# Raw rows scattered straight from X, slots normalised where they are read, six shared groups ahead of the routed part

## The chip, the cores and the metric

One Trainium2 chip, one core of it. The metric is the device time of one execution in microseconds; the kernel before has a median of 673.12 us over 3 runs (672.82 to 673.82).

## The reference, cut to what matters

Two layers over x of shape (2, 2048, 256), float32. First an attention whose scores are distances of 3-component positions (16 heads share one score matrix), then a mixture-of-experts block, which is where the change lies:

```python
x = x + attention(layernorm(x))
xt = layernorm(x)                                   # 4096 rows of 256
scores = softmax(xt @ gate_w.T)                     # 8 experts
_, idx = top_k(scores + gate_bias, 2)
weights = take_along_axis(scores, idx)
for e in range(8):
    gate_e = sum(where(idx == e, weights, 0))
    h = silu(xt @ w1[e].T) * (xt @ w3[e].T)
    y = y + gate_e * (h @ w2[e].T)                  # the routed part
z = silu(xt @ sw1.T) * (xt @ sw3.T) @ sw2.T         # the shared part, inner width 512
x = x + y + z
```

## The kernel before, in words

The 4096 rows are 32 tiles of 128 rows. X, with one tile per index, stays in SBUF through both layers. Every product is made of three matmuls (high by high, high by low, low by high part), so every operand is split: ScalarE copies the rounded high part, VectorE subtracts it for the low part. Each engine has its own hand-written program; semaphores tie them, and within an engine the written order is the order of the work. The second layer has these stages, each named by what the engines' functions are called.

**Logits.** GpSimd makes constants; VectorE folds the statistics of 32 tiles (`mv`), ScalarE takes the square root (`std`), VectorE normalises four tiles at a time into XN (`logits_xn`, line 974 in the helper `normalised`). TensorE transposes XN (L1217), ScalarE and VectorE split the transposed tiles (L858, L985), TensorE multiplies by the gate and turns the result (L1234).

**Router.** VectorE runs a chain of small operations over [128, 32, 8] (from L1047): softmax, two picks, a count per expert, and the slot of every row. Each operation waits for the one before (`done`). Then `choice_weights` gathers the two weights of a row into `meta`.

**Shared part ahead.** A group is four tiles (512 rows) and has four steps n, one per 128 of the inner width. In step n TensorE does `products(n)` (12 matmuls of 512 columns), then `outputs(n - 1)` (12 of 256 columns), and once per group the transposes of the next group (L1258, 8 matmuls). ScalarE does silu (`sg`), the high part of h (L891), and for n < 16 the high part of one of the 16 pieces of the experts' weights (W_hi, L911). VectorE does h (`hf`, L1138), its low part (`h_lo`, L1149), the low part of W (`W_lo`, L1153), and once per group four normalisations (XN), two low parts (XT_lo, L1019) and two additions of the shared output to X (`add_shared`, L1129). HALF = 5 groups run before the routed part. Between `hf` and `h_lo` VectorE also prepares one or two tiles for the scatter (`scatter_tile`): it normalises a tile into a buffer XR (L974) and copies two extra columns, home row and weight (L1108); ScalarE copies the row for the second choice (`second_row`, L898). GpSimd scatters each to DRAM by an indirect DMA (L827), 64 in all, into `slots_in`, where rows of one expert lie in tiles of 128 slots.

**Routed part.** 71 slot tiles. SP loads one into XS (four buffers, next load when TensorE has transposed it and GpSimd has copied its two columns, L833 and L834). TensorE transposes it (L1329), multiplies by the two gate matrices, transposes h (L1345), and multiplies by the third; ScalarE and VectorE split and combine (L933, L1183, L929, L1179, L924, L1174); ScalarE writes the weighted result (L941), GpSimd scatters it home (L843).

**Tail.** SP loads both routed results of every row into YG (L789, 16 DMAs); the remaining 3 groups of the shared part run (12 steps). In seven of their steps, between `hf` and `h_lo`, VectorE adds the two routed results of a group to each other (L1116, two operations) and to X (L1121, two operations): `add_routed`; the eighth group is added at the very end. SP writes tiles out (L794).

The lines that set the split of the work:

```python
HALF = 5
def tiles_to_scatter(n):
    return range(min(2 + 5 * n // 3, NT), min(2 + 5 * (n + 1) // 3, NT))
def group_to_add(n):
    return {2: [0], 3: [1], 4: [2], 5: [3], 6: [4], 7: [5], 9: [6]}.get(n - MC * HALF, [])
```

## Time and profile before

| | |
|---|---|
| median of 3 runs | 673.12 us |
| the profiled execution, its time | 675.16 us |
| its span, first to last instruction | 673.4 us |
| mean granted TensorE clock | 0.921 of full |
| TensorE matmul busy | 560.7 us, 83% |
| VectorE busy | 448.1 us, 67% |
| ScalarE busy | 338.5 us, 50% |
| GpSimd busy | 216.4 us, 32% |

The stages in the trace, in us from the start of the span: attention to 260, logits and router to 319, shared part ahead to 425, routed part to 608, tail to the end. "Idle before" in brackets is how long the engine had nothing to do ahead of a row, and the releaser is what ended that. A matmul's end is modelled, and neighbouring matmuls overlap, so the distance between two starts says what one costs.

### The profile page before, as it was taken

The numbers are of one execution on the slowest core, as the hardware profiler recorded it, in microseconds if no ns is written. First come the engines' busy times: TensorE is split into PE (matmuls) and PEld (weight loads), VectorE is DVE, ScalarE is ACT, GpSimd is POOL, SyncE is SP. The second block draws the span as 40 slices with busy tenths as digits, with TensorE's granted clock in tenths as the row PEclk, the third lists the DMA queues.
The fourth block names the chain that finished last, engine by engine and source line by source line (L and its number), as shares of the span: only waits on it lengthen the run. The fifth ranks groups of instructions, "written<-read, shape, count | busy, mean of one in ns | idle before, by whom it ended". The sixth has DMA issues, their size and how long they took to land.

```text
span 673.4 us, 11259 instructions
## 1 busy us (share of the span) xinstructions
PE 560.7 (83%) x3484; PEld 485.8 (72%) x3484; DVE 448.1 (67%) x1143; ACT 338.5 (50%) x710; POOL 216.4 (32%) x404
## 2 busy tenths in 40 slices
PE   3738899965698994952797989899999999998995
PEld 2727489964658994541676777688888888887884
DVE  4984997888399765967775775444444444444985
ACT  0416998333499851641444444355555555553331
POOL 3061300034132001001774776154545545452000
PEclk9778999968797997977797999899999999999998
DMA  8988000000000004700221222233333333325941
GB/s 280 318 249 3 1 1 1 2 1 0 1 0 1 2 1 149 320 1 8 87 96 55 83 92 87 72 103 103 104 111 103 103 104 104 110 80 174 385 162 62
DMA packets 57127, 62.59 MB, mean 93 GB/s; under 512 B 14736, under 2 KB 50448, under 8 KB 57072
## 3 DMA queue, kind: packets, MB, share of 16 engines
q1 hardware_dynamic: 49216, 43.46, 22.7%
q0 software_dynamic: 6480, 17.77, 7.4%
q10 hardware_dynamic: 1376, 0.66, 0.4%
q8 instruction: 31, 0.51, 0.3%
q14 instruction: 24, 0.20, 0.1%
HBM read 30.50 MB, written 31.37 MB: 92 GB/s over the span
## 4 chain that ended last, share of the span: by engine, by line
PE 40%; DVE 11%; issue 4%; ACT 4%; DVEq 1%; another core or an unknown queue 1%; POOL 0%; ACTq 0%; POOLq 0%
PE bank L1208 11%; PE bank L1210 11%; PE bank L1209 11%; PE bank L1329 2%; PE bank L1345 2%; DVE hf L1138 2%; PE bank L1217 1%; ACT h_hi L891 1%; DVE X L1129 1%; DVE XR L974 1%; DVE h_lo L1149 1%; ACT W_hi L911 1%; DVE XN L974 1%; DVE W_lo L1153 1%; DVE XT_lo L1019 1%
## 5 line engine op out<-in xcount | busy, mean ns | idle before, releaser
L843 POOL DMA_INDIRECT token_out<-YS,to_row x71 | 69.6, 980 | 96.6 <-ACT YS L941 93.0
L827 POOL DMA_INDIRECT slots_in<-XR,slot x64 | 69.4, 1085 | 88.1 <-DVE XR L1108 69.8
L575 PE MATMUL a_bank<-VO,E_hi 128*128 128x258 f32 x272 | 78.6, 289 | 6.6 <-DVE E_lo L482 6.6
L579 PE MATMUL a_bank<-VO,E_lo 128*128 128x258 f32 x272 | 78.2, 288 | 0.0
L577 PE MATMUL a_bank<-VO,E_hi 128*128 128x256 f32 x272 | 78.0, 287 | 0.0
L1179 DVE TENSOR_TENSOR hr<-bank,sr 128x256 f32<-128x256 f32 x71 | 30.1, 425 | 62.0 <-issue 48.9
L1208 PE MATMUL bank<-XT_hi,sw_hi 128*128 128x512 f32 x128 | 53.6, 419 | 13.2 <-DVE XT_lo L1019 11.6
L1208 PE MATMUL bank<-W_hi,XST_hi 128*128 x142 | 62.3, 438 | 0.5 <-DVE XST_lo L1183 0.5
L929 ACT ACTIVATE sr<-bank 128x256 f32<-128x256 f32 x71 | 27.2, 383 | 64.2 <-PE bank L1210 63.4
L575 PEld LDWEIGHTS a_bank<-VO,E_hi 128*128 128x128 f32 x272 | 52.9, 194 | 7.3 <-DVE E_lo L482 7.3
L1210 PE MATMUL bank<-W_hi,XST_lo 128*128 x142 | 56.9, 401 | 0.0
L1209 PE MATMUL bank<-W_lo,XST_hi 128*128 x142 | 56.7, 399 | 0.0
L1208 PE MATMUL bank<-sw_hi,h_hi 128*128 128x256 f32 x128 | 37.5, 293 | 22.7 <-DVE h_lo L1149 18.0
L1183 DVE TENSOR_TENSOR XST_lo<-bank,XST_hi 128x256 fp32r<-128x256 f32 x71 | 30.1, 424 | 38.0 <-ACT XST_hi L933 37.9
L453 DVE TENSOR_SCALAR E<-a_bank 128x512 f32<-128x512 f32 (+3 forms) x80 | 41.6, 598 | 20.5 <-PE a_bank L565 20.5
L579 PEld LDWEIGHTS a_bank<-VO,E_lo 128*128 128x128 f32 x272 | 52.9, 194 | 0.0
L577 PEld LDWEIGHTS a_bank<-VO,E_hi 128*128 128x128 f32 x272 | 52.8, 194 | 0.0
L1210 PE MATMUL bank<-XT_hi,sw_lo 128*128 128x512 f32 x128 | 52.5, 410 | 0.0
L1209 PE MATMUL bank<-XT_lo,sw_hi 128*128 128x512 f32 x128 | 52.4, 409 | 0.0
L482 DVE TENSOR_TENSOR E_lo<-E,E_hi 128x512 fp32r<-128x512 f32 (+1 forms) x80 | 46.0, 603 | 3.9 <-ACT E_hi L299 3.9
L1208 PE MATMUL bank<-W_hi,hT_hi 128*128 x142 | 45.8, 323 | 0.1
L1208 PEld LDWEIGHTS bank<-sw_hi,h_hi 128*128 128x128 f32 x128 | 24.7, 193 | 27.9 <-DVE h_lo L1149 22.2
(227 smaller groups left out, 1621.3 us busy)
## 6 DMA issues: line engine op xcount, KB each, us to landing
XS<-slots_in SPq DMA_DIRECT2D x71, 129.0 KB
YG<-token_out SPq DMA_DIRECT2D x16, 512.0 KB, 7.7
slots_in<-blank SPq DMA_DIRECT2D x7, 1161.0 KB, 14.6
W_raw<-in_wT_dram SPq DMA_DIRECT2D x8, 768.0 KB, 12.5
X<-in_x_dram SPq DMA_DIRECT2D x8, 512.0 KB, 7.7
out_dram<-X SPq DMA_DIRECT2D x32, 128.0 KB, 2.3
token_out<-YS,to_row POOLq DMA_INDIRECT x71, 2.4
slots_in<-blank SPq DMA_DIRECT2D x1, 1032.0 KB, 14.6
```

The costliest lines, as they stand in the source:

```text
L453: dve.tensor_scalar(blk, Q_ps[n % NQ][:, 0:w], 0.0, None, ALU.max).then_inc(s_e2, 1)
L482: dve.tensor_tensor(E_lo[:, n % NE, 0:w], blk, E_hi[:, n % NE, 0:w].bitcast(f32), ALU.subtract).then_inc(s_el, 1)
L575: pe.matmul(O_ps[Q % 2][j][:, 0:D + 2], E_hi[:, n % NE, cols], VO[:, kt, 0:D + 2], start=(kt == 0), stop=False)
L577: pe.matmul(O_ps[Q % 2][j][:, 0:D], E_hi[:, n % NE, cols], VO[:, kt, D + 2:VW], start=False, stop=False)
L579: mm = pe.matmul(O_ps[Q % 2][j][:, 0:D + 2], E_lo[:, n % NE, cols], VO[:, kt, 0:D + 2], start=False, stop=(kt == qt))
L827: pool.indirect_dma_start(out=xs, out_offset=bass.IndirectOffsetOnAxis(ap=slot[k][:, t:t + 1], axis=0), in_=XR[:, t % 4, k, :], in_offset= ...
L843: pool.indirect_dma_start(out=ys, out_offset=bass.IndirectOffsetOnAxis(ap=to_row[:, i:i + 1], axis=0), in_=YS[:, i % NYS, :], in_offset=No ...
L1179: dve.tensor_tensor(hr[:, v, :], S_ps[v][:, D:2 * D], sr[:, v, :], ALU.mult).then_inc(s_hr, 1)
L1183: dve.tensor_tensor(XST_lo[:, v, :, :], XT_ps[v][:, 0:D].rearrange("p (c n) -> p c n", c=KC), XST_hi[:, v, :, :].bitcast(f32), ALU.subtrac ...
L1208: pe.matmul(out, a_hi, b_hi, start=start, stop=False, **kw)
L1209: pe.matmul(out, a_hi, b_lo, start=False, stop=False, **kw)
L1210: return pe.matmul(out, a_lo, b_hi, start=False, stop=stop, **kw)
```

## The change

1. A row of X becomes 262 columns wide: 256 of data, then mean, reciprocal deviation, number of the first choice (FIRST), home row (HOME), second weight (W1), difference of the weights (DW). VectorE fills these in the router. GpSimd scatters rows of X itself, raw, twice; XR, `scatter_tile`, `second_row` and `meta` are gone.
2. The logits are made of raw X: TensorE transposes X, and the router corrects the logits by mean, the sum of the gate's columns (`gsum`, two small matmuls) and the reciprocal deviation. `logits_xn` is gone, the loops over the groups are written out on TensorE and VectorE, and the square root stands behind the first two groups on ScalarE. The choice weights are made before the slots are announced.
3. In the routed part VectorE normalises a slot tile into XSN and compares FIRST with the tile's expert (`slot_rows`: three operations, 71 times); GpSimd makes home row and weight of it by four small operations where there were two.
4. HALF = 6. Two groups are left for the tail. GpSimd adds the two routed results of a row (16 operations of 128x512), VectorE only adds that sum to X. Groups 5 and 6 are both added in the last step.

```diff
-RW = D + 2
+RW = D + 6
+MEAN, RSTD, FIRST, HOME, W1, DW = range(D, RW)
...
-        HALF = 5
+        HALF = 6
...
-            return {2: [0], 3: [1], 4: [2], 5: [3], 6: [4], 7: [5], 9: [6]}.get(n - MC * HALF, [])
+            return {2: [0], 3: [1], 4: [2], 5: [3], 6: [4], 7: [5, 6]}.get(n - MC * HALF, [])
...
 SyncE
             for i in range(4, NSLOT):
-                sp.wait_ge(s_xsT, i - 3)
+                sp.wait_ge(s_sn, i - 3)
                 sp.wait_ge(s_mt, 2 * (i - 3))
...
 GpSimd
             for t in range(NT):
                 for k in range(TOPK):
-                    if k == 0:
-                        pool.wait_ge(s_xr, 2 * t + 2)
-                    else:
-                        pool.wait_ge(s_xr1, t + 1)
                     pool.indirect_dma_start(out=xs,
                                             out_offset=bass.IndirectOffsetOnAxis(ap=slot[k][:, t:t + 1], axis=0),
-                                            in_=XR[:, t % 4, k, :], in_offset=None).then_inc(s_sc[t % 4], 16)
+                                            in_=X[:, t, :], in_offset=None).then_inc(s_sc[t // GT], 16)
 
             def meta_of(i):
+                row = XS[:, i % 4, :]
                 pool.wait_ge(s_xs[i % 4], 16 * (i // 4) + 16)
-                pool.tensor_copy(to_row[:, i:i + 1], XS[:, i % 4, D:D + 1]).then_inc(s_mt, 1)
-                pool.tensor_copy(by_weight[:, i:i + 1], XS[:, i % 4, D + 1:RW]).then_inc(s_mt, 1)
+                pool.wait_ge(s_sel, 2 * i + 2)
+                pool.tensor_tensor(home[:, i:i + 1], back[:, i:i + 1], row[:, HOME:HOME + 1], ALU.add).then_inc(s_meta, 1)
+                pool.tensor_tensor(by_weight[:, i:i + 1], is_first[:, i:i + 1], row[:, DW:DW + 1], ALU.mult)\
+                    .then_inc(s_meta, 1)
+                pool.wait_ge(s_meta, 2 * i + 2)
+                pool.tensor_copy(to_row[:, i:i + 1], home[:, i:i + 1]).then_inc(s_mt, 1)
+                pool.tensor_tensor(by_weight[:, i:i + 1], by_weight[:, i:i + 1], row[:, W1:W1 + 1], ALU.add)\
+                    .then_inc(s_mt, 1)
...
+            for g in range(NG):
+                pool.wait_ge(s_yg[g], 16 * TOPK)
+                for h in range(0, GT, 2):
+                    tiles = slice(g * GT + h, g * GT + h + 2)
+                    pool.tensor_tensor(YG[:, tiles, 0, :], YG[:, tiles, 0, :], YG[:, tiles, 1, :], ALU.add)\
+                        .then_inc(s_yy, 1)
...
 VectorE, router
             dve.wait_ge(s_lg, NG + 2)
+            done(dve.tensor_tensor(tmp[:, :, :], mv[:, :, 0:1].to_broadcast([P, NT, NX]), over_t(gsum), ALU.mult))
+            done(dve.tensor_tensor(logit[:, :, :], logit[:, :, :], tmp[:, :, :], ALU.subtract))
+            done(dve.tensor_tensor(logit[:, :, :], logit[:, :, :], over_e(rstd), ALU.mult))
...
+            for k, out in ((1, X[:, :, W1]), (0, X[:, :, DW])):
+                done(dve.tensor_tensor(tmp[:, :, :], pick[k][:, :, :], score[:, :, :], ALU.mult))
+                done(dve.tensor_reduce(out, tmp[:, :, :], AX.X, ALU.add))
+            done(dve.tensor_tensor(X[:, :, DW], X[:, :, DW], X[:, :, W1], ALU.subtract))
+            dve.wait_ge(s_cols, 3)
             dve.sem_inc(s_slot, 1)
...
 VectorE, add_routed and add_shared
-                dve.wait_ge(s_yg[g], 16 * TOPK)
                 dve.wait_ge(s_zf, 2 * g + 2)
                 for h in range(0, GT, 2):
                     tiles = slice(g * GT + h, g * GT + h + 2)
-                    dve.tensor_tensor(YG[:, tiles, 0, :], YG[:, tiles, 0, :], YG[:, tiles, 1, :], ALU.add)\
-                       .then_inc(s_yy, 1)
-                for h in range(0, GT, 2):
-                    tiles = slice(g * GT + h, g * GT + h + 2)
                     dve.wait_ge(s_yy, g * 2 + h // 2 + 1)
...
+                dve.wait_ge(s_sc[G], 16 * TOPK * GT)
...
 VectorE, routed part
+            def slot_rows(i):
+                dve.wait_ge(s_xs[i % 4], 16 * (i // 4) + 16)
+                if i >= 2:
+                    dve.wait_ge(s_xsT, i - 1)
+                row = XS[:, i % 4, :]
+                dve.tensor_scalar(XSN[:, i % 2, :], row[:, 0:D], row[:, MEAN:MEAN + 1], row[:, RSTD:RSTD + 1],
+                                  ALU.subtract, ALU.mult).then_inc(s_sn, 1)
+                dve.tensor_scalar(is_first[:, i:i + 1], row[:, FIRST:FIRST + 1], which[:, i:i + 1], None,
+                                  ALU.is_equal).then_inc(s_sel, 1)
+                dve.tensor_scalar(back[:, i:i + 1], row[:, FIRST:FIRST + 1], which[:, i:i + 1], -float(P * NT),
+                                  ALU.is_equal, ALU.mult).then_inc(s_sel, 1)
...
+            slot_rows(0)
             for i in range(-3, NSLOT):
+                if i + 4 < NSLOT:
+                    slot_rows(i + 4)
                 if i + 3 < NSLOT:
                     tokens_lo(i + 3, (i + 3) % 2)
```

How the rows move, at three places. First VectorE in a step of the shared part ahead that also normalises the next group (XR is the scatter buffer, XN the next group's tiles). Before:

```order
L1138 TENSOR_TENSOR hf<-bank,sg 128x512
L974 TENSOR_SCALAR XR<-X,mv,rstd 128x256
L1108 COPY XR<-meta 128x2x2
L974 TENSOR_SCALAR XR<-X,mv,rstd 128x256
L1108 COPY XR<-meta 128x2x2
L1149 TENSOR_TENSOR h_lo<-hf,h_hi 128x512
L1153 TENSOR_TENSOR W_lo<-W_raw,W_hi 128x768
L974 TENSOR_SCALAR XN<-X,mv,rstd 128x256 x4
```

The same step of the changed kernel, and the one behind it:

```order
L1126 TENSOR_TENSOR hf<-bank,sg 128x512
L1134 TENSOR_TENSOR h_lo<-hf,h_hi 128x512
L1138 TENSOR_TENSOR W_lo<-W_raw,W_hi 128x768
L973 TENSOR_SCALAR XN<-X,mv,rstd 128x256 x4
L1126 TENSOR_TENSOR hf<-bank,sg 128x512
```

The four rows between `hf` and `h_lo` are gone, the rest stands as it was. Second, VectorE in one turn of the routed part of the changed kernel (XST_lo, hr and hT_lo were there before, in this order and alone):

```order
L1155 TENSOR_TENSOR hT_lo<-bank,hT_hi 128x256
L1167 TENSOR_SCALAR XSN<-XS 128x256
L1169 TENSOR_SCALAR is_first<-XS,which 128x1
L1171 TENSOR_SCALAR back<-XS,which 128x1
L1176 TENSOR_TENSOR XST_lo<-bank,XST_hi 128x256
L1160 TENSOR_TENSOR hr<-bank,sr 128x256
```

Three rows now stand between the low part of h and that of the next slot tile. Third, VectorE in the last two steps of the tail and behind them; before:

```order
L1138 TENSOR_TENSOR hf<-bank,sg 128x512
L1149 TENSOR_TENSOR h_lo<-hf,h_hi 128x512
L1138 TENSOR_TENSOR hf<-bank,sg 128x512
L1149 TENSOR_TENSOR h_lo<-hf,h_hi 128x512
L1129 TENSOR_TENSOR X<-X,bank 128x512 x2
L1116 TENSOR_TENSOR YG<-YG 128x2x256 x2
L1121 TENSOR_TENSOR X<-X,YG 128x512 x2
```

and in the changed kernel:

```order
L1126 TENSOR_TENSOR hf<-bank,sg 128x512
L1107 TENSOR_TENSOR X<-X,YG 128x2x256 x2
L1134 TENSOR_TENSOR h_lo<-hf,h_hi 128x512
L1126 TENSOR_TENSOR hf<-bank,sg 128x512
L1107 TENSOR_TENSOR X<-X,YG 128x2x256 x4
L1134 TENSOR_TENSOR h_lo<-hf,h_hi 128x512
L1117 TENSOR_TENSOR X<-X,bank 128x2x256 x2
L1107 TENSOR_TENSOR X<-X,YG 128x2x256 x2
```

The additions of YG to YG have left VectorE, and four additions to X stand between the last `hf` and the last `h_lo`, where nothing stood.

## Rows read from the trace of the kernel before

**Rows 1.** Windows: two stages; then TensorE, weight loads, VectorE, ScalarE, GpSimd busy, clock, DMA.

```profile
317.00:425.00 108.00, 88.93 (x488) 75.69 (x488) 72.41 (x155) 51.07 (x97) 70.33 (x70) 0.92 0.24 84
425.00:608.00 183.00, 181.88 (x1124) 158.46 (x1124) 83.31 (x212) 98.82 (x281) 87.42 (x204) 0.99 0.33 98
```

**Rows 2.** Line L1138 (`hf`) in the stage ahead, and in the tail.

```profile
L1138 DVE TENSOR_TENSOR hf<-bank,sg x20: 676/683/693, 319.5 to 420.2; 128x512 f32<-128x512 f32 x20
...
L1138 DVE TENSOR_TENSOR hf<-bank,sg x12: 679/692/693, 616.4 to 663.3; 128x512 f32<-128x512 f32 x12
```

**Rows 3.** Timeline of the tail: start us, us, engine, line, operation [idle before].

```profile
614.21 19.41 SPq L789 DMA_DIRECT2D YG<-token_out  x16
...
618.98 0.69 DVE L1138 TENSOR_TENSOR hf<-bank,sg 128x512 f32<-128x512 f32 x1 [0.53 <-PE bank L1210]
623.09 0.69 DVE L1138 TENSOR_TENSOR hf<-bank,sg 128x512 f32<-128x512 f32 x1 [0.74 <-issue]
```

**Rows 4.** The chain that ended last: start us, us, what.

```profile
330.67 0.69 DVE hf L1138
...
642.44 0.87 PE bank L1258 x8
```

**Rows 5.** Timeline, one step of the stage ahead.

```profile
371.25 0.68 DVE L1138 TENSOR_TENSOR hf<-bank,sg 128x512 f32<-128x512 f32 x1
...
373.26 0.69 DVE L1149 TENSOR_TENSOR h_lo<-hf,h_hi 128x512 fp32r<-128x512 f32 x1 [0.80 <-issue]
374.00 0.96 DVE L1153 TENSOR_TENSOR W_lo<-W_raw,W_hi 128x768 fp32r<-128x768 f32 x1
374.07 1.73 POOL L827 DMA_INDIRECT slots_in<-XR,slot  x1 [0.30 <-issue]
374.88 1.38 DVE L974 TENSOR_SCALAR XN<-X,mv,rstd 128x256 f32<-128x256 f32 x4
```

**Rows 6.** Timeline, the head of the logits.

```profile
261.77 2.22 DVE L967 BATCH_NORM_AGGREGATE mv<-st 128x2 f32<-128x6 f32 x32 [2.09 <-POOL before L815]
264.07 1.28 ACT L851 ACT_TABLE_LOAD   x1 [14.80 <-DVE mv L967]
267.59 3.32 PE L1217 MATMUL bank<-ident,XN 128*128 128x128 f32 x16 [9.42 <-DVE XN L974]
...
273.43 0.39 PE L1208 MATMUL bank<-XT_hi,gate_hi 128*8 128x512 f32 x1
```

**Rows 7.** Timeline, the end of the router and the first step.

```profile
314.50 0.42 DVE L1101 TENSOR_TENSOR tmp<-pick,score 128x256 f32<-128x256 f32 x1 [0.15 <-DVE slot L1088]
...
319.53 0.69 DVE L1138 TENSOR_TENSOR hf<-bank,sg 128x512 f32<-128x512 f32 x1 [2.31 <-ACT sg L885]
...
324.21 0.58 PE L1208 MATMUL bank<-sw_hi,h_hi 128*128 128x256 f32 x1 [16.15 <-DVE h_lo L1149]
```

**Rows 8.** Timeline, ScalarE's longest unexplained wait in the stage ahead.

```profile
356.39 1.09 ACT L879 ACTIVATE XT_hi<-bank 128x512 fp32r<-128x512 f32 x2 [3.02 <-remote]
```

**Rows 9.** Timeline, one turn of the routed part.

```profile
500.71 0.41 DVE L1174 TENSOR_TENSOR hT_lo<-bank,hT_hi 128x256 fp32r<-128x256 f32 x1
...
501.66 0.42 DVE L1183 TENSOR_TENSOR XST_lo<-bank,XST_hi 128x256 fp32r<-128x256 f32 x1 [0.54 <-ACT XST_hi L933]
...
503.37 0.47 PE L1208 MATMUL bank<-W_hi,XST_hi 128*128 x1
```

**Rows 10.** Timeline of the attention, GpSimd adding while VectorE works.

```profile
40.33 4.83 POOL L252 TENSOR_TENSOR X<-X,shift 128x256 f32<-128x256 f32 x7
...
41.84 0.67 DVE L413 TENSOR_TENSOR l<-pos,h 128x48 f32<-128x48 f32 x1
44.58 0.20 DVE L418 TENSOR_REDUCE nrm<-t 128x16 f32<-128x48 f32 x1
```

**Rows 11.** Line L1116: the additions of YG to YG, and the landing of YG.

```profile
L1116 DVE TENSOR_TENSOR YG<-YG x16: 677/683/693, 623.7 to 668.5; 128x512 f32<-128x512 f32 x16
...
DMA to landing us min/median/max: 4.1/7.7/8.8
```

More of the change, by code:

```diff
@@ L241, in _ @@
             pool.wait_ge(s_const, 8)
+            pool.memset(blank[:, FIRST:FIRST + 1], -1.0).then_inc(s_const, 1)
             pool.affine_select(out=ident[:, :], in_=ident[:, :], compare_op=ALU.not_equal, fill=1.0, base=0,
@@ L605, in attention_and_experts @@
         gbias = sb("gbias", [P, NX])
+        ones_f = sb("ones_f", [P, P])
+        gsum = sb("gsum", [P, NX])
         logit = sb("logit", [P, NT, NX])
@@ L613, in attention_and_experts @@
         red2 = sb("red2", [P, NT])
-        meta = sb("meta", [P, NT, TOPK, 2])
+        biased = sb("biased", [P, NT, NX])
+        slot_e = sb("slot_e", [P, NT, NX])
+        total = sb("total", [P, NX, NT])
+        upto = sb("upto", [P, NX, NT])
+        keep = sb("keep", [P, NX, NT])
+        passed = sb("passed", [P, NSLOT, NX])
+        is_first = sb("is_first", [P, NSLOT])
+        back = sb("back", [P, NSLOT])
+        home = sb("home", [P, NSLOT])
         to_row = sb("to_row", [P, NSLOT], u32)
@@ L716, in attention_and_experts @@
         s_slot = sem("f_slot")
-        s_xr = sem("f_xr")
-        s_sc = [sem(f"f_sc{i}") for i in range(4)]
+        s_sc = [sem(f"f_sc{g}") for g in range(NG)]
+        s_gs = sem("f_gs")
+        s_gsum = sem("f_gsum")
+        s_cols = sem("f_cols")
+        s_sel = sem("f_sel")
+        s_sn = sem("f_sn")
         s_wr = sem("f_wr")
@@ L775, in _ @@
             sp.wait_ge(s_T, N_T + KC * HALF)
-            for k in range(4):
-                sp.wait_ge(s_sc[k], 16 * TOPK * NT // 4)
+            for g in range(NG):
+                sp.wait_ge(s_sc[g], 16 * TOPK * GT)
             for k in range(4):
@@ L844, in _ @@
                                         in_=YS[:, i % NYS, :], in_offset=None).then_inc(s_yst[i % NYS], 16)
+            for g in range(NG):
+                pool.wait_ge(s_yg[g], 16 * TOPK)
[3 more added lines that the diff above has]
+                        .then_inc(s_yy, 1)
         @block.scalar
@@ L903, in shared @@
                         gate_silu(n)
-                        if G < HALF:
-                            for t in tiles_to_scatter(n):
-                                second_row(t)
                         chunk_hi(n)
@@ L975, in normalised @@
                                          ALU.subtract, ALU.mult)
-            def logits_xn(G, v):
-                for j in range(GT):
-                    normalised(XN[:, v, j, :], G * GT + j).then_inc(s_xn, 1)
             def logits_lo(G, v):
@@ L1061, in _ @@
                 if k + 1 < TOPK:
+                    dve.tensor_scalar(X[:, :, FIRST], red2[:, :], -1.0, float(NX), ALU.mult, ALU.add).then_inc(s_cols, 1)
+                    dve.wait_ge(s_cols, 3)
                     done(dve.scalar_tensor_tensor(out=biased[:, :, :], in0=pick[k][:, :, :], scalar=-3.0e38,
@@ L1097, in slot_experts @@
                 dve.sem_inc(s_slot, 1)
-            def choice_weights():
-                for k in range(TOPK):
-                    done(dve.tensor_tensor(tmp[:, :, :], pick[k][:, :, :], score[:, :, :], ALU.mult))
-                    done(dve.tensor_reduce(meta[:, :, k, 1], tmp[:, :, :], AX.X, ALU.add))
-            def scatter_tile(t):
-                if t >= 4:
-                    dve.wait_ge(s_sc[t % 4], 16 * TOPK * (t // 4))
-                normalised(XR[:, t % 4, 0, 0:D], t).then_inc(s_xr, 1)
-                dve.tensor_copy(XR[:, t % 4, :, D:RW], meta[:, t, :, :]).then_inc(s_xr, 1)
             def add_routed(g):
-                dve.wait_ge(s_yg[g], 16 * TOPK)
                 dve.wait_ge(s_zf, 2 * g + 2)
@@ L1141, in shared @@
                             slot_experts()
-                        if G < HALF:
-                            for t in tiles_to_scatter(n):
-                                scatter_tile(t)
-                        else:
+                        if G >= HALF:
                             for g in group_to_add(n):
@@ L1222, in logits @@
                 pe.wait_ge(s_xtl, G * KC + 3 * KC)
-                if not (isinstance(G, int) and G == 0):
+                if G > 0:
                     pe.wait_ge(s_lc, G)
@@ L1240, in _ @@
             logits_transpose(1, 1)
+            for c in range(KC):
+                mm = pe.matmul(gs_ps, ones_f[:, :], gate_raw[:, c, :], start=(c == 0), stop=(c == KC - 1))
+            mm.then_inc(s_gs, 1)
             logits(0, 0)
-            with pe.Fori(0, NG // 2 - 1) as k:
-                for v in range(2):
-                    logits_transpose(k * 2 + v + 2, v)
-                    logits(k * 2 + v + 1, 1 - v)
-                    turn_logits(v)
+            pe.wait_ge(s_gsum, 1)
+            for G in range(NG - 2):
+                logits_transpose(G + 2, G % 2)
+                logits(G + 1, 1 - G % 2)
+                turn_logits(G % 2)
             logits(NG - 1, 1)
```

117 lines of the change are left out of this document (47 added, 70 removed).

## The prediction

> **What bounds the kernel now.** I read the windows by stage first, then line L1138, whose operation `hf` beats once per step of the shared part, then timelines. In the routed part TensorE is busy 181.9 of 183.0 us at a granted clock of 0.99 [rows 1]: it is the bound, 2.58 us for each of 71 slot tiles. In the stage ahead it is busy 88.9 of 108 us, clock 0.92: something else holds it. The steps say how much [rows 2]. Ahead, 19 steps take 420.2 - 319.5 = 100.7 us, 5.3 each; in the tail 11 take 46.9, 4.27 each. What TensorE alone needs is seen where VectorE waits for it: `hf` to `hf` is 623.09 - 618.98 = 4.11 us [rows 3], I use 4.12, and once per group 0.9 us of transposes come on top [rows 4]. The tail's 11 steps would need 2.6 (the first, with no outputs in it) + 10 x 4.12 + 2 x 0.9 = 45.6 us: the tail is bound by TensorE but for 1.3 us. Ahead, VectorE is the bound [rows 5]: from `hf` to `h_lo` go 2.01 us, of which 0.8 idle, since one scatter tile stands between (in most steps it is two), then 0.74 to W_lo, 0.9 for that, 1.4 for the XN. That is 5.1 us for a step of 4.12.
>
> **The change, part by part,** against the profiled span of 673.4 us. That execution's own time is 675.16, the median of the runs 673.12; I take the sum of differences off the median. About 0.2% (1.3 us) is what a measurement of this kernel can tell from no change.
>
> *Head of the logits.* VectorE starts at 261.77 when GpSimd's constants are done; TensorE's first transpose comes at 267.59, behind `mv` (2.2), the table load (1.3), the square root and the XN [rows 6]. Now transposes of raw X need only the constants: 262.1, two small ones later. I follow it at half clock, which rows before show here (16 transposes in 3.3 us): group 0 done 263.8; `gate_lo` comes after `mv` at 264.6 and TensorE waits for it, then group 1 until 266.3; products of group 0 from 266.6. The next products need ScalarE's copy behind table load and root (266.95 + 1.6 + 0.6) = 269.2, where they now stand at 273.43. Gain 4.2, and 0.2 over six further groups, since TensorE paces them as before: **-4.4**.
>
> *Router.* Three operations more for the correction at 0.45 each, 0.42 of it busy [rows 7], 0.25 for FIRST, 0.2 for the subtraction: +1.8. After 314.5 + 4 x 0.46 = 316.3, where the weights are done, VectorE prepared two tiles and waited for ScalarE, which copied them, loaded Silu's table and made `sg`: `hf` came at 319.53. ScalarE now does all that while the router runs; -3.3. With the above, the first `hf` is at 319.5 - 4.4 + 1.8 - 3.3 = 313.6: **-5.9** in all.
>
> *First steps.* TensorE's first outputs came 4.7 us after that `hf` [rows 7], because ScalarE and VectorE had scatter rows to make; now 3.0 (slot_experts stays between, 1.7). `hf` number 2 came 11.1 us after number 0 [rows 4]; now 3.0 + 2.6 + 3.5 = 9.2, the first 4 us at half clock as before: **-1.9**.
>
> *Stage ahead.* From `hf` 2 to `hf` 19 were 420.2 - 330.7 = 89.5 us. Without the scatter rows VectorE's longest step is 0.62 + 0.75 + 0.62 + 0.15 + 0.9 + 1.4 = 4.4, and over a group's four steps it needs less than TensorE's 17.4: TensorE is the bound. To `hf` 23: 21 x 4.12 + 5 x 0.9 = 91.0. I add 3 for what is not smooth; the stage also holds a stall of ScalarE that no row explains, 3.0 us with low clock behind it [rows 8], which may come again or not. 94.0 - 89.5 = **+4.5**, so a whole group more costs that little. GpSimd now scatters without waiting: 64 x 1.4 us = 90, done long before 24 steps are; an addition of group G waits for 8(G + 1) scatters, 11 us a group against 17.4. So this wait is free. Bounds: 0 and 10 for the allowance.
>
> *Routed part.* Between hT_lo and XST_lo stand three operations more, 0.33 + 2 x 0.2 us. XST_lo started at 501.66, would start at about 501.85 and end at 502.3, where TensorE wants it at 503.37 [rows 9]. The cover is 1.1 us per turn; so nothing per turn, and **+0.5** once for the first tile's normalisation in front of its transpose. GpSimd's two more small operations (0.2 each) and their wait lie in its idleness, (183 - 87.4) / 71 = 1.3 us per turn [rows 1]. Were the cover gone, each 0.1 us would cost 7 us.
>
> *Tail.* Eight steps: 2.6 + 6 x 4.12 + 0.9 = 28.2 from first to last `hf`, against 46.9. But GpSimd now adds, and the attention shows what that does [rows 10]: while GpSimd runs additions of 0.68 us one behind the other, VectorE's operations on [128, 48] with two SBUF inputs take 0.67 where the same size with one (L418) takes 0.20; they end when GpSimd's instruction does, and GpSimd is not slowed. Its indirect DMA behaves the other way: it stretches from 0.96 to 1.73 beside W_lo, and VectorE keeps its time [rows 5]. By the Trainium skill (GPSIMD Engine Reference, Key points) GpSimd shares its SBUF interfaces with VectorE and contends with VectorE instructions in a 2-port mode or with two SBUF inputs; the trace agrees on which instructions suffer, 0.67 against 0.20, and adds who yields.
>
> An addition of 512 columns I take as 2 x 0.68 less a bit, 1.3 us, estimated from the 256-column one; the bounds are 0.68 and 1.4. The results land group by group from about 620.5 to 640 [rows 3, 11], 2.7 us apart, so GpSimd's 16 additions fill that stretch. In it VectorE does, each behind one GpSimd addition: four XN (5.9 us instead of 1.4), then in each step two additions to X and one `h_lo`, 3 x 1.9 + 0.6 for `hf` = 6.3 us and 1.3 more where XT_lo or the shared output is added. Written out step by step on the old clock, `hf` of the eight steps falls at 616.4, 619.0, 626.9, 633.6, 639.0, 645.7, 649.3, 653.4, where TensorE alone would give 644.6 for the last: +8.8. So 37.0 us instead of 46.9: **-9.9** (bounds: -18.7 with no hold, -5 if every operation is held in full).
>
> *End.* Four additions to X (2.6 us) now stand between the last `hf` and `h_lo`, of which 0.7 was idle: +1.9. The two YG additions behind it are gone, 2 x 0.64 [rows 11]: -1.3. **+0.6**.
>
> Sum: -5.9 - 1.9 + 4.5 + 0.5 - 9.9 + 0.6 = -12.1; 673.1 - 12.1 = **661 us**, 1.8% less.
>
> **The rivals.**
> (a) *GpSimd's additions don't hold VectorE, or in short stretches only.* For: the operations held in the attention were short ones, the tail's are long. Against: seven in a row were held. Then the tail is TensorE's and the result is 661 - 8.8 = **652**. Read as mere sharing, the skill's rule would give something near this. Chance 0.22.
> (b) *The stage ahead stays with VectorE and ScalarE* for the 16 steps that split W. For: W_hi and W_lo are in series with `h_hi` and `h_lo`, and the steps that run at 4.1 to 4.2 before have no W in them. Against: my count of a group, 17.4. Four steps take 20.3 us before; if half of the 2.9 excess stays in four groups, +6, if all of it, +12, each less the 3 allowed: **664 to 670**, still faster. Chance 0.12.
> (c) *The routed turn grows, and the kernel is slower.* Place: VectorE between hT_lo and XST_lo, and the chain slot_rows, four GpSimd operations, SP's load into one of four buffers. Price 7 us per 0.1 us and turn; it decides from 12.1 / 71 = 0.17 us per turn. With 0.25 us it gives 661 + 18 = **679**. Against: 1.1 us of cover [rows 9] and over one turn of slack on the load. Chance 0.06.
> (d) *The scatter lies not where I say:* raw scatters back to back delay the shared additions by their landing. An addition late by one group's landing costs up to 5 us in all: **up to 666**, inside the forecast's bounds and counted there. Against: 11 us a group against 17.4.
>
> **How the numbers follow.** Forecast with (d) 0.60, with 656 to 667 for its own bounds (allowance, hold of 4 to 13); (a) 0.22, (b) 0.12, (c) 0.06. The range from 650 to 669 leaves out (c), the end of (b) and the corners of (a). Slower by over 0.2%: 0.05; within: 0.03; faster 0.92.
>
> **What would show it.** Right: first `hf` near 313.6; steps ahead at 4.1 to 4.4 us; routed part 183 to 185 us with TensorE over 98% busy; in the tail additions to X, XN and `h_lo` at 1 to 2 us each beside GpSimd's additions of about 1.3, `hf` to `hf` 5 to 7 us there, and 4.1 once GpSimd is done. Wrong: VectorE's operations in the tail at 0.68 (then (a)); steps with W at 5 us (b); a turn of 2.7 us (c).

## The result: 715 us, slower, against a forecast of 661

The changed kernel takes 715.25 us (median of four runs: 710.8, 714.0, 716.5, 723.8), the kernel before beside it 673.47. The ratio, which leaves out the run of 723.8 us as a slow one, is 1.059, with a 95% interval of 1.053 to 1.065. The profiled execution took 716.48, with a span of 714.0 us.

The page's second part (busy tenths in 40 slices of 17.85 us) shows where. Slices 19 to 27 are the shared stage ahead (the rows are TensorE and GpSimd busy, and TensorE's granted clock):

```profile
PE   3829899693989979439522499989999999999875
...
POOL 3052200305220010037777200015777777776590
PEclk9969999886999989859855599999999999999999
```

In slices 21 and 22 TensorE is busy for two tenths, and its clock is at half. GpSimd has four slices of 7 there, 19 to 22: these are the scatters. The windows over the same time (columns as in [rows 1]):

```profile
320.00:340.00 20.00, 18.92 (x108) 16.37 (x108) 11.46 (x19) 8.38 (x14) 15.75 (x14) 0.98 0.27 95
340.00:400.00 60.00, 19.77 (x79) 14.89 (x78) 8.71 (x14) 5.70 (x9) 44.41 (x45) 0.62 0.29 103
400.00:420.00 20.00, 15.22 (x68) 12.47 (x69) 10.03 (x17) 7.46 (x12) 0.00 (x0) 0.76 0.00 0
...
425.00:470.00 45.00, 45.00 (x265) 39.81 (x265) 26.77 (x43) 17.79 (x29) 0.00 (x0) 1.00 0.05 13
...
480.00:655.00 175.00, 175.00 (x1091) 152.82 (x1090) 117.19 (x409) 95.87 (x273) 121.10 (x333) 1.00 0.33 100
```

Between 340 and 400 TensorE, VectorE and ScalarE all nearly stand, only GpSimd goes on. GpSimd's last scatter ends at 397.9. From 400 to 420 the others recover, from 425 on TensorE is busy 45 us out of 45, and in the routed part 175 out of 175. The steps are told by `hf`; its first, its number 2 and 23 (stage ahead), and number 24 and 31 (tail), from the timeline of VectorE:

```profile
312.68 0.69 DVE L1126 TENSOR_TENSOR hf<-bank,sg 128x512 f32<-128x512 f32 x1 [0.24 <-DVE X L1089]
322.74 0.69 DVE L1126 TENSOR_TENSOR hf<-bank,sg 128x512 f32<-128x512 f32 x1 [1.51 <-ACT sg L900]
471.75 0.69 DVE L1126 TENSOR_TENSOR hf<-bank,sg 128x512 f32<-128x512 f32 x1 [2.10 <-PE bank L1206]
667.97 0.69 DVE L1126 TENSOR_TENSOR hf<-bank,sg 128x512 f32<-128x512 f32 x1 [3.34 <-PE bank L1206]
703.25 0.69 DVE L1126 TENSOR_TENSOR hf<-bank,sg 128x512 f32<-128x512 f32 x1 [2.10 <-ACT sg L900]
```

This splits the change of the span, 714.0 - 673.4 = +40.6 us, into the terms of the forecast:

| stretch | before | after | measured | forecast |
|---|---|---|---|---|
| start to first `hf` | 319.5 | 312.7 | -6.8 | -5.9 |
| first steps, `hf` 0 to 2 | 11.1 | 10.1 | -1.1 | -1.9 |
| stage ahead, `hf` 2 to 19 or 23 | 89.5 | 149.0 | **+59.5** | +4.5 |
| last `hf` ahead to first of the tail | 196.2 | 196.2 | 0.0 | +0.5 |
| tail, first to last `hf` | 47.0 | 35.3 | -11.7 | -9.9 |
| last `hf` to the end | 10.1 | 10.7 | +0.7 | +0.6 |

Five of six terms are within 2 us. One is off by 55 us. The stall in the timelines of VectorE and ScalarE:

```profile
345.08 0.69 DVE L1134 TENSOR_TENSOR h_lo<-hf,h_hi 128x512 fp32r<-128x512 f32 x1 [0.70 <-ACT h_hi L906]
355.03 0.96 DVE L1138 TENSOR_TENSOR W_lo<-W_raw,W_hi 128x768 fp32r<-128x768 f32 x1 [9.26 <-issue]
...
376.26 0.69 DVE L1126 TENSOR_TENSOR hf<-bank,sg 128x512 f32<-128x512 f32 x1 [19.07 <-issue]
...
404.88 0.69 DVE L1126 TENSOR_TENSOR hf<-bank,sg 128x512 f32<-128x512 f32 x1 [25.54 <-ACT sg L900]
...
344.42 0.63 ACT L906 ACTIVATE h_hi<-hf 128x512 fp32r<-128x512 f32 x1 [1.67 <-DVE hf L1126]
351.52 0.60 ACT L894 ACTIVATE XT_hi<-bank 128x512 fp32r<-128x512 f32 x1 [6.47 <-remote]
```

ScalarE's XT_hi at 351.52 is the plainest row: ScalarE was free from 345.05, TensorE's transposes that it reads were made by 344, and yet it starts 6.5 us later. TensorE's own queue and GpSimd's at the depth of the stall:

```profile
386.69 0.29 PEld L1206 LDWEIGHTS bank<-sw_hi,h_lo 128*128 128x128 f32 x1 [2.50 <-issue]
388.10 0.37 PE L1206 MATMUL bank<-sw_hi,h_lo 128*128 128x256 f32 x1 [2.44 <-issue]
389.49 0.29 PEld L1204 LDWEIGHTS bank<-XT_hi,sw_hi 128*128 128x128 f32 x1 [2.51 <-issue]
390.89 0.59 PE L1204 MATMUL bank<-XT_hi,sw_hi 128*128 128x512 f32 x1 [2.42 <-issue]
...
394.43 0.96 POOL L828 DMA_INDIRECT slots_in<-X,slot  x1 [0.30 <-issue]
395.69 0.96 POOL L828 DMA_INDIRECT slots_in<-X,slot  x1 [0.30 <-issue]
396.96 0.96 POOL L828 DMA_INDIRECT slots_in<-X,slot  x1 [0.31 <-issue]
```

TensorE starts one instruction per 1.4 us, weight load and matmul in turn, "issue" in front of each: none of them waits for anything that the profile shows. GpSimd starts a scatter per 1.27 us, to the last one at 396.96. Some us later everything recovers. The half clock is a consequence: from 340 to 350, when the stall begins, the granted clock (third column from the end) was still 1.00, and it fell once TensorE stood:

```profile
340.00:350.00 10.00, 8.77 (x51) 7.21 (x50) 4.21 (x8) 1.82 (x3) 7.78 (x8) 1.00 0.30 107
350.00:360.00 10.00, 2.75 (x7) 2.18 (x8) 2.16 (x3) 1.93 (x3) 7.56 (x9) 0.57 0.28 100
```

### The profile page after: what moved, and what is told of

The parts are those of the page before. It is cut to its first block, busy times and chain, and to the rows that moved or that the text cites. A ratio compares the mean times of both kernels' runs of the same rounds, so it can differ in the third digit from the quotient of the medians.

```text
span 714.0 us, 11544 instructions
## 1 busy us (share of the span) xinstructions
PE 568.0 (80%) x3488; PEld 489.9 (69%) x3488; DVE 468.0 (66%) x1252; ACT 329.1 (46%) x678; POOL 273.9 (38%) x564
## 4 chain that ended last, share of the span: by engine, by line
PE 46%; issue 8%; DVE 7%; ACT 1%; DVEq 0%; POOL 0%; another core or an unknown queue 0%; POOLq 0%; ACTq 0%
PE bank L1204 14%; PE bank L1206 13%; PE bank L1205 13%; PE bank L1327 2%; PE bank L1343 2%; PE bank L1212 1%; DVE h_lo L1134 1%; PE bank L1256 1%; DVE XN L973 1%; DVE hf L1126 1%; DVE sw_lo L1019 0%; DVE X L1117 0%; DVE X L1107 0%; DVE mv L970 0%; PE bank L1229 0%
## 5 line engine op out<-in xcount | busy, mean ns | idle before, releaser
L828 POOL DMA_INDIRECT slots_in<-X,slot x64 | 65.9, 1029 | 72.0 <-DVEq L1091 52.8
L852 POOL DMA_INDIRECT token_out<-YS,to_row x71 | 71.9, 1012 | 47.9 <-DVE back L1171 43.9
L1204 PE MATMUL bank<-sw_hi,h_hi 128*128 128x256 f32 x128 | 38.4, 300 | 40.6 <-DVE h_lo L1134 17.9
L1126 DVE TENSOR_TENSOR hf<-bank,sg 128x512 f32<-128x512 f32 x32 | 22.0, 689 | 68.1 <-ACT sg L900 35.3
L906 ACT ACTIVATE h_hi<-hf 128x512 fp32r<-128x512 f32 x32 | 20.2, 632 | 85.1 <-DVE hf L1126 85.1
L577 PEld LDWEIGHTS a_bank<-VO,E_hi 128*128 128x128 f32 x272 | 52.1, 192 | 7.8 <-DVE E_lo L484 7.8
L579 PEld LDWEIGHTS a_bank<-VO,E_hi 128*128 128x128 f32 x272 | 52.1, 192 | 0.0
L900 ACT ACTIVATE sg<-bank 128x512 f32<-128x512 f32 x32 | 19.1, 597 | 64.0 <-PE bank L1206 49.8
```

Of the source, the lines that this page charges most:

```text
L577: pe.matmul(O_ps[Q % 2][j][:, 0:D + 2], E_hi[:, n % NE, cols], VO[:, kt, 0:D + 2], start=(kt == 0), stop=False)
L579: pe.matmul(O_ps[Q % 2][j][:, 0:D], E_hi[:, n % NE, cols], VO[:, kt, D + 2:VW], start=False, stop=False)
L828: pool.indirect_dma_start(out=xs, out_offset=bass.IndirectOffsetOnAxis(ap=slot[k][:, t:t + 1], axis=0), in_=X[:, t, :], in_offset=None).th ...
L852: pool.indirect_dma_start(out=ys, out_offset=bass.IndirectOffsetOnAxis(ap=to_row[:, i:i + 1], axis=0), in_=YS[:, i % NYS, :], in_offset=No ...
L1126: dve.tensor_tensor(hf[:, n % 2, :], U_ps[n % 2][:, :], sg[:, n % 2, :], ALU.mult).then_inc(s_hf, 1)
L1204: pe.matmul(out, a_hi, b_hi, start=start, stop=False, **kw)
```

## The experiments

The theory: 64 indirect DMAs issued back to back stall the other engines, and the small stall of ScalarE before the change [rows 8], which came at the end of ten scatters in a row, was the same thing. Rivals: the wider raw rows, the place of the instructions in the program, the moment.

### Set 1: pauses between scatters

The paced kernel waits for `hf` of the step as the kernel before did through its XR buffers:

```diff
             for t in range(NT):
+                if t >= 2:
+                    pool.wait_ge(s_hf, 3 * (t - 2) // 5 + 1)
                 for k in range(TOPK):
```

`e1_paced`: 

> The changed kernel, but GpSimd waits for `hf` of the steps before it scatters the next tiles, at the rate of the kernel before (five tiles per three steps, at most four scatters in a row). Theory A, the unbroken run of 64 scatters is what stalls the other engines from 345 to 399 us: the steps take 4.1 to 4.4 us throughout, hf number 23 comes 94 to 98 us after number 2 and the time is 660 to 667 us. Theory B, it is something else in the new stage ahead (raw rows of 1048 bytes, reads of X beside VectorE, the additions' wait for the scatter): 700 us or more.

`e2_late` (one `pool.wait_ge(s_hf, 4)` ahead of the loop): 

> The changed kernel, but the 64 scatters begin only when `hf` number 3 is there (15 us later), unbroken as before. Theory A with the length of the run as its measure: other engines run well for the first 30 us of scatters and stall behind, so the stall now begins near 360 instead of 345 and ends with the scatters near 412 to 415; time 700 to 720 us. Theory C, the place in the program (a certain step, its code or its semaphores) sets the stall: it begins at 345 as it did.

`e3_filler` (a memset of one column ahead of each scatter): 

> The changed kernel, but a memset of one column stands between any two scatters, without a wait: GpSimd is as unbroken as it was, one scatter comes per 1.6 us instead of 1.27. If what counts is GpSimd without a pause, the stall is longer than before (scatters until about 415) and the time is 725 us or more; if what counts is the rate of scatters (a backlog that grows by what they come too fast), the stall begins far later or never, and the time is 660 to 690 us.

`e4_runs16` (`if t >= 8: pool.wait_ge(s_hf, 6 * (t // 8))`): 

> The changed kernel, but the scatters come in four runs of 16 (20 us each), which begin when `hf` number 5, 11 and 17 are there. Theory A with a run length of about 25 scatters before others stall: no stall, 660 to 670 us. If even 16 in a row are too many, stalls of some us at the end of each run, 675 to 700 us. Theory B: 700 us or more.

Measured: **659.5 us** (658.5 to 661.6, ratio 0.986, interval 0.980 to 0.992), 667.9, 660.2 and 661.5 us. None stalls. From 340 to 400 us of the paced kernel:

```profile
340.00:400.00 60.00, 60.00 (x360) 53.32 (x359) 40.84 (x65) 28.33 (x45) 45.09 (x43) 1.00 0.28 99
```

`hf` number 23 comes at 414.5, 92.2 us after number 2, where I had forecast 94.0. But this set proves less than it seems. The waits of the paced kernel were nearly always met before GpSimd reached them. The page of the changed kernel and that of `e1_paced`:

```profile
L828 POOL DMA_INDIRECT slots_in<-X,slot x64 | 65.9, 1029 | 72.0 <-DVEq L1091 52.8
L830 POOL DMA_INDIRECT slots_in<-X,slot x64 | 67.3, 1051 | 73.0 <-DVEq L1093 53.8
```

Behind the first scatter (52.8 and 53.8 us of idle time are in front of it) GpSimd is idle for 19.2 us in both, 0.30 a scatter: `e1_paced` scattered here without a break, from 311.7 to 397.2. `e2_late` issues 64 scatters without any wait between them, from 329.7 to 415.1, and but for one wait TensorE is busy throughout:

```profile
350.00:415.00 65.00, 65.00 (x388) 57.66 (x387) 43.00 (x68) 29.86 (x48) 50.51 (x48) 1.00 0.28 100
```

Its 8 us over `e1_paced` are one wait for the late scatters (an addition to X at 342.63 stands 7.95 us). And the kernel before took 671.0 us in this set (666.1 to 671.9), less than beside the changed one. Only `e4_runs16` had real pauses (4.4 to 6.3 us from scatter to scatter). Either any small shift cures the stall, or it did not come on this chip at all. The changed kernel itself was not in the set, a mistake in its design.

### Set 2: the same scatters from another place, at another moment

```diff
+            for j in range(40):
+                pool.memset(junk[:, j:j + 1], 0.0)
             pool.wait_ge(s_slot, 1)
```

`m1_code_moved`: 

> The changed kernel with 40 memsets of one column more on GpSimd, done while it waits for the slots (it was idle for 52 us there): the 64 unbroken scatters are the same and begin at the same moment, only their instructions stand 40 places further on. Theory A2, the unbroken scatters stall the others by themselves wherever they stand: 705 to 725 us. Theory D, the stall needs a certain coincidence of where the instructions of the engines stand in their code (and so when each engine has to fetch more): it is gone or moved, 658 to 690 us.

`m2_begin_later` (`pool.wait_ge(s_hf, 1)` ahead of the loop): 

> The changed kernel, but the 64 unbroken scatters begin with the first `hf` instead of with the last slot, about 1 us later or not at all. Theory A2: 705 to 725 us. Theory D with the moment as what coincides: gone or moved, 658 to 690 us.

Measured on a second chip, one run each: **723.5** and **728.0 us**, the kernel before 673.9. A small shift cures nothing. TensorE first stands for over 1.5 us at 337.2 and at 330.6 us instead of 349.8, and goes again 5 to 11 us behind the last scatter, so neither the place nor the moment makes the stall. In the second, TensorE's matmul at 364.90 had stood 20 us:

```profile
344.35 0.49 PE L1207 MATMUL bank<-XT_hi,sw_lo 128*128 128x512 f32 x1 [0.33 <-issue]
364.90 0.55 PE L1205 MATMUL bank<-sw_hi,h_hi 128*128 128x256 f32 x1 [20.05 <-issue]
```

### Sets 2 and 3: who sums the pairs, and pacing where the stall comes

`t1_vector_sums` has the pacing of `e1_paced`, and VectorE sums YG as before the change; `t2_mixed_sums` does that for `g < 5` and leaves groups 5 to 7 to GpSimd.

```diff
 GpSimd
-            for g in range(NG):
-                pool.wait_ge(s_yg[g], 16 * TOPK)
...
 VectorE, add_routed
                 dve.wait_ge(s_zf, 2 * g + 2)
+                if g < 8:
+                    dve.wait_ge(s_yg[g], 16 * TOPK)
+                    for h in range(0, GT, 2):
+                        tiles = slice(g * GT + h, g * GT + h + 2)
+                        dve.tensor_tensor(YG[:, tiles, 0, :], YG[:, tiles, 0, :], YG[:, tiles, 1, :], ALU.add)\
+                           .then_inc(s_yy, 1)
```

> The kernel with paced scatters (659.5 us), but VectorE sums the routed pairs as before the change, GpSimd adds nothing in the tail. If GpSimd's additions cost the tail by holding VectorE's operations (they take 1.06 to 1.78 us instead of 0.68): `hf` of the eight steps spans 30 to 32 us instead of 35.2, and the end behind it is 2 to 3 us longer (groups 5, 6 and 7 are summed there), so 656.5 to 659 us. If the sums' own time on VectorE costs as much as the hold: 660 us or more.

> The kernel with paced scatters, VectorE sums groups 0 to 4, GpSimd the last three (six additions instead of sixteen). The holds are then few and late: `hf` of the eight steps spans 31 to 33 us and the end stays at 10.8: 656 to 658 us. If any hold in the last steps costs in full: 659 us or more.

Both missed: **673.1** (668.3 to 676.2) and **675.6 us** (671.0 to 679.0), level with the kernel before, since the coarse pacing does not keep the stall away in this set: `hf` 0 to 23 takes 118 and 123 us instead of 103. Their tails are free of it and are read on their own below. Set 3, on a third chip, had the changed kernel in it:

`c1_changed_again`: 

> The changed kernel once more, as the control of this set. The first four experiments ran on a chip where the kernel before took 671.0 us, the next four on one where it took 673.9; unbroken scatters stalled nothing on the first and 723 to 728 us were measured on the second. Theory E, whether the stall comes is a matter of the chip: where the kernel before takes about 674 us the changed one takes 705 to 728, where it takes about 671 the changed one takes 657 to 662.

`e1_again`: 

> The kernel with scatters paced by the steps (659.5 us on the chip without the stall), beside the control. On a chip without the stall: 658 to 661 us again. On a chip with it: the stages of the two kernels with VectorE's sums and the same pacing say 8 to 12 us more, 666 to 674 us, stalls of 3 to 8 us behind runs of 10 to 16 scatters, which end because the steps that stand also stop the scatters.

`f1_even`: 

> The changed kernel, but every scatter waits for an event of its own, three per step (`hf`, `h_lo`, `sg` of the next), so one comes per 1.2 to 1.6 us, and none runs ahead of the steps. On a chip with the stall: if a backlog of scatters that come every 1.27 us is its cause, it is gone, 658 to 664 us; if their mean rate over the stage is already too much, 666 to 674 as with the coarse pacing. On a chip without it: 658 to 661.

`f2_filler3`: 

> The changed kernel, but three memsets of one column stand between any two scatters, none of which waits for a step: one scatter per 1.5 to 1.6 us, unbroken for 100 us. On a chip with the stall: if the rate is what counts, no stall, 658 to 666 us; if it is that the scatters go on whatever the steps do, 700 us or more. On a chip without it: 658 to 664.

```diff
                 for k in range(TOPK):
+                    c = TOPK * t + k
+                    n = c // 3
+                    if c % 3 == 0:
+                        pool.wait_ge(s_hf, n + 1)
+                    elif c % 3 == 1:
+                        pool.wait_ge(s_hl, n + 1)
+                    else:
+                        pool.wait_ge(s_sg, n + 2)
```

Measured: changed kernel **725.7**, coarse pacing **675.8** (672.8 to 682.4, ratio 1.004, interval 1.001 to 1.008; above its 666 to 674), one scatter per event **666.0** (665.7 to 666.1, ratio 0.988, interval 0.985 to 0.991), filler **725.1**; the kernel before 674.0. The windows 340 to 400 of the changed kernel, of `f1_even` and of the filler:

```profile
340.00:400.00 60.00, 8.39 (x24) 6.10 (x24) 3.72 (x5) 1.96 (x3) 41.76 (x43) 0.53 0.27 98
```

```profile
340.00:400.00 60.00, 54.85 (x324) 48.11 (x323) 37.31 (x60) 25.32 (x41) 40.10 (x38) 1.00 0.24 84
```

```profile
340.00:400.00 60.00, 29.26 (x90) 21.09 (x91) 9.71 (x15) 6.48 (x10) 49.88 (x165) 0.61 0.26 94
```

The changed kernel stalls here, for 66 us (`hf` 0 to 23 in 168.9 instead of 102.9), so the occasion decides whether the stall comes, and the edit how much it can cost. The filler stretches the scatters to one per 1.41 us (314.8 to 403.9) and does not help. Waits on the steps do, and their effect is a feedback: a step that stands stops the scatters, and the stall ends after 3 to 8 us. Even so the stage ahead of `e1_again` takes 106.3 us from `hf` 2 to 23 and that of `f1_even` 99.5, where 92.2 were seen without a stall. The longest stand of `f1_even` is at the same operation as in [rows 8] and as long as there:

```profile
345.81 1.09 ACT L902 ACTIVATE XT_hi<-bank 128x512 fp32r<-128x512 f32 x2 [2.98 <-remote]
```

### Set 4: bytes, issuing, or the missing feedback

`x2_short_rows` (`out=xs_short`, `in_=X[:, t, 0:8]`, and the rows for empty slots are numbered from 0 on; the routed part has only blank rows to work on):

> The changed kernel with unbroken scatters, but each writes rows of 32 bytes instead of 1048 (from X into a tensor of its own; the routed part then works on blank rows, so the routed products are left out of the result). GpSimd issues the same 64 instructions at the same pace, the queue moves one thirtieth of the bytes. On a chip with the stall: if the issuing (GpSimd's own work for the descriptors) stalls the others, 700 us or more as before; if the bytes or packets on the queue do, no stall and 650 to 665 us.

`x3_group_by_group`:

```diff
             for t in range(NT):
+                if t >= GT and t % GT == 0:
+                    pool.wait_ge(s_sc[t // GT - 1], 16 * TOPK * GT)
```

> The changed kernel, but GpSimd waits after each eight scatters until these have landed (2 to 3 us), and for no step. On a chip with the stall: if it is a backlog that the unbroken run builds up over more than ten scatters, these pauses clear it and the time is 658 to 670 us; if what helps is only that scatters stop when the steps stand, 700 us or more.

`f1_again`: 

> The kernel with one scatter per event of a step, once more, as the control of this set: 665 to 667 us on a chip where the changed kernel stalls, 657 to 660 on one where it doesn't.

This set ran on the chip of set 1. `f1_again` took 666.2 us (661.0 to 670.8) and the kernel before 673.2, so the stall came here now: it does not belong to a chip for good. Short rows: **725.7 us**. The next to last column of the window is the DMA share, 0.03 instead of 0.29:

```profile
340.00:400.00 60.00, 8.77 (x26) 6.25 (x25) 4.85 (x7) 3.65 (x6) 43.65 (x45) 0.56 0.03 3
```

The bytes are out, and with them the wider rows; the packets of the scatters' queue were 1472 in this window against 2208, so their number is not out. Pauses without any feedback from the steps: **664.4 us**, one run. Runs of eight scatters, 2.7 to 3.3 us from the start of the last to the start of the next, and TensorE is busy for 59.87 of 60 us, `hf` 0 to 23 in 104.7:

```profile
340.00:400.00 60.00, 59.87 (x353) 52.82 (x352) 40.82 (x66) 27.31 (x44) 41.44 (x38) 1.00 0.25 88
```

TensorE's longest stand between 315 and 420 is 1.1 us. So a feedback from the steps is not needed: a break before a run of scatters gets long is enough, as far as this one run shows, beside the stalling run of the short rows. It costs the scatters 13 us in all (they end at 409.9 instead of 397), and no addition to X waits for them.

### The tail, and a faster kernel

GpSimd's additions and VectorE beside them, timeline of the changed kernel:

```profile
673.07 4.29 DVE L973 TENSOR_SCALAR XN<-X,mv,rstd 128x256 f32<-128x256 f32 x4
677.28 0.68 DVE L1126 TENSOR_TENSOR hf<-bank,sg 128x512 f32<-128x512 f32 x1
677.88 2.96 DVE L1107 TENSOR_TENSOR X<-X,YG 128x512 f32<-128x512 f32 x2
680.77 1.76 DVE L1134 TENSOR_TENSOR h_lo<-hf,h_hi 128x512 fp32r<-128x512 f32 x1
682.45 1.27 DVE L1011 TENSOR_TENSOR XT_lo<-bank,XT_hi 128x512 fp32r<-128x512 f32 x2
...
677.32 6.37 POOL L858 TENSOR_TENSOR YG<-YG 128x512 f32<-128x512 f32 x4 [0.43 <-DMA YG<-token_out]
```

and the groups of its tail, from 655 us to the end (count, busy, mean ns of one, idle before):

```profile
L1107 DVE TENSOR_TENSOR X<-X,YG 128x512 f32<-128x512 f32 x16 | 16.2, 1058 | 0.1
L1134 DVE TENSOR_TENSOR h_lo<-hf,h_hi 128x512 fp32r<-128x512 f32 x8 | 9.2, 1155 | 1.4 <-ACT h_hi L906 1.4
...
L858 POOL TENSOR_TENSOR YG<-YG 128x512 f32<-128x512 f32 x16 | 24.8, 1576 | 8.5 <-DMA YG<-token_out 8.5
```

XN (1.38 us for four before), the additions to X (0.68 each) and `h_lo` (0.69) are held to 4.29, 1.5 and 1.76 us. `hf` and XT_lo, which read one operand from PSUM, are not: 0.68 and 0.64. By the Trainium skill (GPSIMD Engine Reference, Key points) VectorE instructions in a 2-port mode or with two SBUF inputs contend with GpSimd. The rows of the additions and of `h_lo`, which have two SBUF inputs, agree; XN has one tensor input and is held as well, and no row shows in which mode it runs. Both sides lose: GpSimd's additions take 1.30 and 1.32 us beside XN (at 674.3 and 675.6), but up to 1.75 us beside the additions to X and `h_lo`. `hf` to `hf` is 6.4, 4.6 and 6.3 us there. `x4_even_vector` has the scatter waits of `f1_even`, gives the sums back to VectorE and reorders the end; of its edit, the order:

```diff
-            return {2: [0], 3: [1], 4: [2], 5: [3], 6: [4], 7: [5, 6]}.get(n - MC * HALF, [])
+            return {2: [0], 3: [1], 4: [2], 5: [3], 6: [4], 7: [5]}.get(n - MC * HALF, [])
...
+                if groups[-1] == NG - 1:
+                    add_routed(NG - 2)
+                    sum_routed(NG - 1)
                 add_shared(groups[-1], 0)
```

`x4_even_vector`: 

> The candidate for a kernel faster than both: one scatter per event of a step, VectorE sums the routed pairs, group 6 is added and group 7 summed behind the last `h_lo`, while TensorE makes the last outputs. From the first `hf` of the tail to the end VectorE's sums took 44.6 us against 47.0 with GpSimd's, and this order takes 1.5 to 2.5 off the end: 3 to 5 us less than the control, 661 to 663 on a chip with the stall, 654 to 656 on one without. If the sums in the last steps hold TensorE instead: the control's time.

| tail | first to last `hf` | last `hf` to end | sum |
|---|---|---|---|
| GpSimd sums (`f1_again`) | 35.2 | 11.4 | 46.6 |
| mixed (`t2_mixed_sums`) | 34.5 | 11.2 | 45.7 |
| VectorE sums (`t1_vector_sums`) | 29.1 | 15.4 | 44.5 |
| VectorE, new order (`x4_even_vector`) | 29.1 | 12.9 | 42.0 |

Measured: **660.4 us** (657.8 to 664.5, ratio 0.982, interval 0.977 to 0.987) beside the control's 666.2 (661.0 to 670.8). The ranges overlap, as both kernels still have stalls of changing length in the stage ahead; what the tail gives is read from the traces, 4.6 us by the table. VectorE's sums alone give 2.1 of them, the new order the rest. Its groups of the tail stand at their own length again:

```profile
L1118 DVE TENSOR_TENSOR X<-X,YG 128x512 f32<-128x512 f32 x16 | 10.3, 684 | 0.1
L1107 DVE TENSOR_TENSOR YG<-YG 128x512 f32<-128x512 f32 x16 | 10.3, 682 | 0.0
...
L1145 DVE TENSOR_TENSOR h_lo<-hf,h_hi 128x512 fp32r<-128x512 f32 x8 | 5.5, 685 | 1.4 <-ACT h_hi L908 1.4
```

Last, on a fourth chip, both helpful parts together, and a filler of 13 small additions in place of each pause of `x3_group_by_group`:

`x5_best`: 

> Both parts that helped: GpSimd waits after each eight scatters for their landing, and VectorE sums the routed pairs with group 6 and 7 behind the last `h_lo`. The stage ahead as with the pauses (104.7 us from first `hf` to number 23, or 103 without any stall) and the tail as in the last candidate (43.6 us from its first `hf`): 657 to 660 us.

`x6_other_work`: 

> The changed kernel, but after each eight scatters GpSimd does 13 small additions (2.5 to 3 us) instead of waiting for the landing: it issues no scatter there, yet is not idle. Where the changed kernel stalls: if a break in the scatters is what helps, 658 to 670 us, as with the waits (664.4); if GpSimd has to be idle, or the landing to be waited for, 700 us or more. Where it doesn't stall: 657 to 662 with a kernel before at 666 to 671.

Measured: **655.4 us** (653.2 to 656.1, six runs; the kernel before beside it 668.8; ratio 0.980, interval 0.977 to 0.983), the fastest version of this study, and below its forecast of 657 to 660. Its stage ahead takes 92.2 us from `hf` 2 to 23, so the pauses cost nothing there, and its tail 42.0. The second took 660.3, with TensorE busy in all 60 us of the window. That settles nothing: the kernel before took 668.8 here and 671.0 in set 1, where the stall did not come, against 673.2 to 674.0 in the sets where it came, so this was most likely an occasion without it, and the changed kernel was not run beside.

## Why the prediction was wrong

*Head of the logits and router: right.* 6.8 us gained, forecast 5.9. But 1.7 of the 6.8 come from the attention, which ended that much earlier: `mv` starts at 260.07 instead of 261.77. The head itself gave 5.1.

*First steps: half right*, 1.1 gained of 1.9.

*Stage ahead: this step failed.* It said: "GpSimd now scatters without waiting: 64 x 1.4 us = 90, done long before 24 steps are ... So this wait is free." The scatters took about what was forecast (312.8 to 397.9, 1.33 each) and the additions' wait was free. But I priced only the waiting for the scatters, not what issuing them does to the engines beside. The waits that the change took from GpSimd were also what tied the scatters to the steps and broke them up: into runs of 16, 10, 10, 10, 10 and 8, if only pauses of over 1 us count. The trace had the sign in it. The stall "that no row explains" [rows 8] stands at the end of the second of these runs, 26 scatters in 37 us with one pause of 1.4 us, and GpSimd's longest wait comes with it:

```profile
354.01 0.96 POOL L827 DMA_INDIRECT slots_in<-XR,slot  x1 [0.30 <-issue]
361.67 0.96 POOL L827 DMA_INDIRECT slots_in<-XR,slot  x1 [6.69 <-DVE XR L1108]
```

I let it come once again or not, within an allowance of 3 us and a bound of 10 for the whole stage. In the five kernels of sets 2 to 4 whose scatters went on unbroken, and in the first run of the changed kernel, it cost 56 to 67 us. None of the rivals held it; each was slower or faster by a wait or a hold, none by a stop of the other engines. Where the stall did not come, the term was right: 92.2 us against 94.0, TensorE bound, a group of four steps in 17.6 us where the count had 17.4. Rival (b) is thereby out.

*Routed part: right.* 196.2 us from `hf` to `hf` as before; the cover of 1.1 us per turn held, so rival (c) is out. *Additions waiting for landings (d): out*, except in `e2_late`, which made them wait on purpose.

*Tail: right in kind, less good in size.* GpSimd's additions hold VectorE, rival (a) is out. The hold costs 35.3 - 28.2 = 7.1 us, forecast 8.8. One addition of GpSimd takes 1.58 us on the average, not 1.3: the 1.3 holds where VectorE does not slow it, and that it would not be slowed, as I read in the attention, was wrong here. On the other side the additions to X beside it take 1.2 to 1.5 us, not 1.9, and the four XN 4.3, not 5.9. What I had not weighed is the other way of doing it: with six groups ahead, VectorE's own sums, in a better order at the end, make the tail 4.6 us shorter.

*Sum.* Without the stall the change gives 659.5 us beside 671.0 (`e1_paced`, whose waits took 0.6 us in all), 11.5 less where 12.1 were forecast; the kernel before has no trace in that set, so the terms cannot be compared there one by one. With the stall, 715 to 728.

Open: why unbroken issuing of indirect DMAs starves the other engines, why on some occasions and not on others, and whether GpSimd has to wait in the break or may work. One rival was not tested, the loading of code. Between 326 and 400 us the two DMA queues that the profile names "instruction" move five packets in `e1_paced` and none in `c1_changed_again`, where the next comes at 403.8 and TensorE goes again at 403.3. Whether the engines stood because code did not come, or no code was asked for because they stood, no run tells.

## What to carry to other kernels

A wait that an engine loses may have been pacing it: before you call the freed engine's work free, ask what it does at full speed to the engines beside it, and take a stand that no row explains for a sign and not for noise: here it came after 26 scatters with one short pause. Break long runs of GpSimd's indirect DMAs, here after eight, by a wait for their landing: it cost nothing where there was no stall, and removed it in the one run where there was. Look whether a wait that you add is ever waited for; that of the paced kernel was not. And put the unchanged kernel under test into every set of runs: a set without it looked like four cures.
